# One fused attention and expert kernel: a new hand-written order of the work of eight images

## The reference

```python
x = x + conv(ln_c(x))            # attention block on the normed input
t = tokens(x)
t = t + ffn(ln_t(t))             # experts on the normed tokens

def conv(x):
    qkv = conv1x1(x)                         # 768 channels
    agg = grouped_1x1(depthwise_5x5(qkv))    # 25 taps per channel
    # 64 heads of 8 channels: 32 from qkv, 32 from agg
    q, k = relu(q), relu(k); v = [v, 1]
    kv = k^T v;  out = q kv;  out = out[:-1] / out[-1]
    return batchnorm(conv1x1(out))

def ffn(x):                                  # per image
    probs = softmax(mean_tokens(x) @ router)
    weights of 6 experts from the best 2 of 11 partitions
    return sum_e w_e * (gelu(x W1_e + b1_e) W2_e + b2_e)
```

## Time and profile before

| | us |
|---|---|
| median of 3 runs | 1727.04 |
| lowest and highest | 1724.31 and 1729.64 |
| the profiled execution | 1725.51 |
| its span, first to last instruction | 1723.6 |

### The profile page before, as it was taken

One profiled execution on the slowest core, in us unless ns is written; L12 is line 12 of the kernel. 1 busy time (PEld: TensorE's weight loads), 2 busy tenths in 40 slices (PEclk: granted clock), 3 DMA queues, 4 the chain that ended last, 5 costly groups with the idle time before them and its releaser, 6 DMA issues.

```text
span 1723.6 us, 18116 instructions
## 1 busy us (share of the span) xinstructions
PE 1403.7 (81%) x6652; PEld 771.5 (45%) x6652; DVE 1303.4 (76%) x1305; ACT 915.0 (53%) x1606; POOL 1187.4 (69%) x1017
## 2 busy tenths in 40 slices
PE   4344865988889878988889878988889879768998
PEld 2133534544545435544545435544445435534443
DVE  4999999889589895889589895889589895920000
ACT  3452642565557644665557645565557645433554
POOL 3673554877697758876697758876697757535776
PEclk7666986999999989999999989999999989988999
DMA  5100000000010000100010000100010000100000
GB/s 173 74 0 25 1 0 0 25 1 13 1 62 1 13 1 0 62 1 13 1 60 3 13 1 1 61 1 13 1 37 1 13 0 1 37 0 13 1 13 25
DMA packets 14247, 32.70 MB, mean 19 GB/s; under 512 B 2384, under 2 KB 5328, under 8 KB 13904
## 3 DMA queue, kind: packets, MB, share of 16 engines
q1 hardware_dynamic: 14160, 31.56, 5.2%
HBM read 23.17 MB, written 8.39 MB: 18 GB/s over the span
## 4 chain that ended last, share of the span: by engine, by line
PE 44%; DVE 23%; POOL 16%; ACT 10%; issue 6%; DMA 1%; POOLq 0%; SPq 0%; DVEq 0%
DVE dacc L1067 19%; PE wbk L487 16%; PE acc L500 12%; PE wbk L580 6%; POOL dwo L881 4%; POOL gl L915 3%; POOL hb L912 3%; ACT tapb L655 2%; POOL yr L905 2%; PE wbk L589 2%; PE wbk L534 2%; POOL nrm L838 1%; PE wbk L539 1%; PE wbk L554 1%; PE wbk L566 1%
## 5 line engine op out<-in xcount | busy, mean ns | idle before, releaser
L1067 DVE SCALAR_TENSOR_TENSOR dacc<-qkvs,dww,dacc 128x930 f32<-128x930 f32 (+4 forms) x954 | 1052.3, 1185 | 0.0
L912 POOL TENSOR_SCALAR hb<-hb,ewg 128x512 f32<-128x512 f32 x256 | 189.8, 742 | 252.2 <-ACT gh L677 252.1
L915 POOL TENSOR_TENSOR gl<-hb,gh 128x512 f16<-128x512 f32 x256 | 306.3, 1196 | 21.4
L770 ACT ACTIVATE hb<-wbk,b1s 128x512 f32<-128x512 f32 x256 | 175.4, 686 | 244.4 <-PE wbk L487 243.8
L881 POOL TENSOR_TENSOR dwo<-dwo,tapb 128x992 f32<-128x992 f32 (+1 forms) x104 | 237.4, 2283 | 46.7 <-ACT tapb L655 39.5
L487 PE MATMUL wbk<-th,w1h 128*128 128x512 f16 x512 | 163.8, 403 | 69.7 <-ACT vt L743 36.7
L500 PE MATMUL acc<-gh,w2h 128*128 128x512 f16 x512 | 200.6, 392 | 19.4 <-POOL gl L915 19.3
L677 ACT ACTIVATE gh<-hb,ewg 128x512 f16<-128x512 f32 x256 | 182.3, 712 | 40.7 <-DVE ewg L1020 40.7
L500 PE MATMUL acc<-gl,w2h 128*128 128x512 f16 x512 | 200.0, 391 | 0.0
L500 PE MATMUL acc<-gh,w2l 128*128 128x512 f16 x512 | 199.8, 390 | 0.0
L487 PE MATMUL wbk<-tl,w1h 128*128 128x512 f16 x512 | 162.3, 400 | 0.0
(11 more groups left out here) (147 smaller groups left out, 2388.7 us busy)
## 6 DMA issues: line engine op xcount, KB each, us to landing
xa<-x SPq DMA_DIRECT2D x8, 1024.0 KB, 5.0
yr<-x SPq DMA_DIRECT2D x8, 1024.0 KB, 5.0
out<-yr SPq DMA_DIRECT2D x16, 512.0 KB, 2.8
dwo<-w SPq DMA_DIRECT2D x1, 2048.0 KB, 10.9
yr<-w SPq DMA_DIRECT2D x2, 1024.0 KB, 16.0
dwo<-w_qkv SPq DMA_DIRECT2D x1, 768.0 KB, 4.7
wp<-w_proj SPq DMA_DIRECT2D x1, 512.0 KB, 12.1
pw<-w_pw SPq DMA_DIRECT2D x16, 24.0 KB
```

Of the source, the lines that this page charges most:

```text
L770: last = nc.scalar.activation(hb[:, f % GB, :], b[:], ACT.Gelu, bias=b1s[:, f % FT:f % FT + 1], scale=1.0 / (X_SCALE * W_SCALE))
L912: nc.gpsimd.tensor_scalar(hb[:, f % GB, :], hb[:, f % GB, :], ewg[s % 2][:, f % FT:f % FT + 1], 0.0, ALU.mult, ALU.add).then_inc(g_scaled, 1)
L915: nc.gpsimd.tensor_tensor(gl[:, f % GB, :], hb[:, f % GB, :], gh[:, f % GB, :], ALU.subtract).then_inc(g_low, 1)
L1067: ins = nc.vector.scalar_tensor_tensor(out=dst[:, oy, ox], in0=i3[:, jy, jx], scalar=dww[:, m, tap:tap + 1], in1=a3[:, oy, ox], op0=ALU.mu ...
```

## The change

Only the list, the items' grain and the places of the small tasks change; every instruction of the computation stays. `high`, `squares`, `relu_q`, `apply`, `low` and `scale` are split into one item for each block or half. `base` items are given one for each `fill` step (three after each banked item in j = 0). `gsplit` is given only once the image's `exp` is given, and so the first two steps of an image may come before its `exp`. The core of the new list:

```diff
+            if todo and ("low", todo[0][0], 1, CT - 1) in given and (("exp", todo[0][0]) in given or todo[0][1] < 2):
+                i = len(stream) - len(todo)
+                give(("ffn",) + todo.pop(0))
+                while unsplit and ("exp", unsplit[0][0]) in given:
+                    give(("gsplit",) + unsplit.pop(0))
+                unsplit.append(stream[i])
+                if i >= LAG:
+                    second(i - LAG)
+            base(1)
...
+    def norm_in(s):
+        return [[("squares", s, 0, 0)], [("squares", s, 0, 1), ("sums", s, 0)],
+                [("stats", s, 0, 0)], [("stats", s, 0, 1), ("rnorm", s, 0)],
+                [("rbc", s, 0, 0), ("rbc", s, 0, 1)], [("apply", s, 0, 0)], [("apply", s, 0, 1)]]
+    def norm_out(s):
+        return [[("high", s, 0, 0)], [("low", s, 0, 0), ("high", s, 0, 1)], [("low", s, 0, 1)]]
...
+    for j in range(B + 1):
+        d, c, a, f = j < B, j >= 1, j + 1 < B, j + 2 < B
+        new, nxt = j - 1, j + 1
         n = 3 if j == 0 else 1
         if c:
+            give(*agg(new, 0), *agg(new, 1))
+            fill(1)
             for t in range(TT):
+                give(("att", new, 1, t))
+                if t == 3:
+                    fill(1)
+                    give(("scale", new, 1, 0))
+            give(("scale", new, 1, 1))
+        if j == 0:
+            for group in norm_in(1)[:2]:
+                give(*group)
         if d:
+            give(*qkv(j, 0), *qkv(j, 1), n=n)
+            add_base(j, 0)
+            if j == 0:
+                for group in norm_in(1)[2:]:
+                    give(*group, n=n)
+        out = norm_out(nxt) if a else [[], [], []]
         if c:
+            fill(2)
+            give(*[("back", new, 1, ch, g) for ch in range(NCH) for g in range(2)])
+            fill(1)
+            give(("proj", new, 0, 0), *out[0])
+            give(("proj", new, 0, 1))
+            give(("proj", new, 1, 0), *out[1])
+            give(("proj", new, 1, 1))
+        else:
+            give(*out[0], *out[1])
+        toks = [("tok", j, t) for t in range(TT)] if d else []
+        give(*toks[:2], n=n)
+        if c:
+            if not d:
+                fill(2)
+            give(*out[2], ("squares", new, 1, 0))
+            give(*toks[2:4])
+            give(("squares", new, 1, 1), ("sums", new, 1))
+            give(*toks[4:])
+        else:
+            give(*out[2], *toks[2:], n=n)
         if d:
+            give(("relu_q", j, 0))
+            give(("kv", j, 0, 0), ("kv", j, 0, 1), n=n)
+            give(("mask", j, 0), ("relu_q", j, 1))
         if c:
+            fill(1)
+            give(("stats", new, 1, 0), ("rnorm", new, 1))
+            fill(1)
         if d:
+            give(*[("att", j, 0, t) for t in range(4)], n=n)
         if c:
+            fill(1 if d else 2)
+            give(("rbc", new, 1, 0), ("rbc", new, 1, 1), ("apply", new, 1, 0), ("apply", new, 1, 1))
+        if d:
+            give(("scale", j, 0, 0))
+            give(*[("att", j, 0, t) for t in range(4, TT)], n=n)
         if c:
+            give(("high", new, 1, 0))
+            fill(1 if d else 2)
+            give(("high", new, 1, 1))
+        if d:
+            give(("scale", j, 0, 1))
+        if c:
+            give(("low", new, 1, 0), ("low", new, 1, 1))
+            if a:
+                give(*qkv(nxt, 2))
+            give(("logits", new))
+        if d:
+            give(*[("back", j, 0, ch, g) for ch in range(NCH) for g in range(2)], n=n)
+        if c:
+            if a:
+                give(*qkv(nxt, 3))
+            else:
+                fill(1)
+            fill(left(new - 1) + 2)
             give(("exp", new))
...
+            give(*agg(j, 2), *agg(j, 3))
...
+            for group in norm_in(j + 2) if f else [[]] * 4:
+                give(*group)
+                fill(1)
+            fill(1)
+            give(*agg(j, 4))
+            fill(1)
+            give(*agg(j, 5))
+            fill(1)
+            if a:
+                for m in (4, 5):
+                    for it in qkv(nxt, m):
+                        give(it)
+                        fill(1)
+                add_base(nxt, 4)
+            else:
+                fill(4)
+            give(("kv", j, 1, 0))
+            fill(2)
+            give(("kv", j, 1, 1))
+            fill(1)
             give(("mask", j, 1))
+            while left(new) > KEEP and new >= 0:
+                fill(1)
...
+KEEP = 9
...
-            OF_LAST = {14: ("rden", 1, 0), 20: ("rden", 1, 1), 74: ("max",), 84: ("route",)}
-            OF_THIS = {94: ("rden", 0, 0), 100: ("rden", 0, 1)}
+            OF_LAST = {10: ("rden", 1, 0), 14: ("rden", 1, 1), 72: ("max",), 80: ("route",)}
+            OF_THIS = {58: ("rden", 0, 0), 64: ("rden", 0, 1)}
```

More of the change, by code:

```diff
@@ L82, in schedule @@
     o = []
+    given = set()
     waiting = []
@@ L85, in schedule, with give, base, rest @@
     todo = list(stream)
[L86 to L90, removed]
+    unsplit = []
+    def give(*items, n=1):
+        for it in items:
+            o.append(it)
+            given.add(it)
+            if it[0] in BANKED and n > 1:
+                base(n)
+    def base(n):
+        o.extend(waiting[:n])
+        del waiting[:n]
+    def rest():
+        base(len(waiting))
+    def add_base(s, a):
+        waiting.extend(("base", s, m, i) for m in (a, a + 1) for i in range(base_taps(s, m)))
     def second(k):
@@ L96, in second, with fill @@
             give(("final", s, n // FT))
-    def fill(k, s):
+    def fill(k):
         for _ in range(k):
[L100 to L130, removed]
@@ new lines, in norm_out @@
+    def norm_out(s):
+        return [[("high", s, 0, 0)], [("low", s, 0, 0), ("high", s, 0, 1)], [("low", s, 0, 1)]]
+    give(("squares", 0, 0, 0), ("squares", 0, 0, 1), ("sums", 0, 0), ("weights", 0), ("stats", 0, 0, 0),
+         ("stats", 0, 0, 1), ("rnorm", 0, 0), ("rbc", 0, 0, 0), ("rbc", 0, 0, 1), ("apply", 0, 0, 0),
+         ("apply", 0, 0, 1), ("weights", 1), ("high", 0, 0, 0), ("low", 0, 0, 0), ("high", 0, 0, 1), ("low", 0, 0, 1))
+    give(*[it for m in range(2, QT) for it in qkv(0, m)])
@@ L135, in schedule @@
+    add_base(0, 2)
+    add_base(0, 4)
+    for j in range(B + 1):
+        d, c, a, f = j < B, j >= 1, j + 1 < B, j + 2 < B
+        new, nxt = j - 1, j + 1
         n = 3 if j == 0 else 1
         if c:
-            agg(new, 0)
-            fill(1, old)
+            give(*agg(new, 0), *agg(new, 1))
+            fill(1)
             for t in range(TT):
[L140 to L143, removed]
@@ L179, in schedule @@
-        if c:
-            give(("exp", new))
-        fill(2, new)
-        if a:
-            based([("stats", j + 1, 0, i) for i in range(2)])
-            give(("rnorm", j + 1, 0))
-            fill(2, new)
-            based([("rbc", j + 1, 0, ch) for ch in range(NCH)])
-            give(("apply", j + 1, 0))
-        if j == -1:
-            give(("weights", 1))
-        if d:
[L191 to L194, removed]
-            give(("scale", j, 0))
@@ new lines, in schedule @@
+        if d:
[6 more added lines that the diff above has]
+            fill(left(new - 1) + 2)
+            give(("exp", new))
+        rest() if j == 0 else None
+        if d:
+            give(*agg(j, 2), *agg(j, 3))
+            if a and c:
+                add_base(nxt, 2)
+        if j == 0:
+            give(*qkv(1, 2), *qkv(1, 3))
+            add_base(1, 2)
@@ L223, in schedule @@
     return o
+KEEP = 9
+BANKED = ("qkv", "agg", "kv", "stats", "rbc", "att", "back", "proj", "tok", "logits", "ffn")
 ORDER = schedule()
-BANKED = ("qkv", "agg", "kv", "stats", "rbc", "att", "back", "proj", "tok", "logits", "ffn")
 FILL = {it: n for n, it in enumerate([it for it in ORDER if it[0] in BANKED])}
@@ L243, in norm_before @@
 def norm_before():
-    runs = [(it[1], it[2]) for it in ORDER if it[0] == "squares"]
+    runs = [(it[1], it[2]) for it in ORDER if it[0] == "squares" and it[3] == 0]
     return dict(zip(runs[1:], runs))
```

141 lines of the change are left out of this document (47 added, 94 removed).

## The result

The new list takes 1774.07 us (1770.77 to 1776.88, four runs), the old one 1727.11 beside it: ratio 1.0272, 95% interval 1.0248 to 1.0296. It is 2.7% slower. The forecast was 1708, and the range ended at 1742.

The account below looks back on a forecast made before the run. Bound: a PE-ACT-POOL loop of fixed-order queues, with VectorE hung on it at the logits. 228 + 187 + 4 x 195 + 175 + 165 + 170 = 1705 us of span, plus 1.9 and 1.5: 1708; range 1640 to 1742.

Parts of the forecast that it names:

- Stage A: From agg of q to the logits: 83 us, against 105.7 before; the wait before `max` goes.
- Stage B: From the logits to the routed weights: 22.5 us, ending at 105.5 in the period; 20.3 before.
- head: Start to the end of the first image's taps: 228 us, against 201.8, as VectorE stands 26 us at `rden`.
- light period: First period after the head, without old steps: 187 us, VectorE's taps setting the route at 100.7.
- j = 7: Last tap period, without qkv or norm: 165 us, against 183.7 before.
- tail: Behind the last tap period, with 9 steps of image 6 left instead of 22: 170 us, against 204.7.
- stage C: From routed weights to the input norm's rbc: 26.5 us, POOL's serial queue making PE stand at three places.
- Rival 2: The slower rival: the stretch behind the route costs more, through half clock, 6 us a period; 1738 us; chance 0.26.
- The third rival: Logits come no earlier; Stage A costs 4 us more in each of four periods; 1724, no change; chance 0.10.
- Stage D: From rbc to the next agg of q: 58.7 us, plus 2.5 for half clock and 1.8 for taps; period 195.
- The period of j = 6: The period without an input norm: 20 us shorter for the norm's missing work, 175 us.
- the rival of the experiments that named PE's clock: Set up for the experiments: PE's own number of items and clock set the period; no size or chance given.

Follow-up runs that it names:

- run 3: Kernel after, with no base items at the steps between the input norm's groups (j of 1 and more): 1729.01 us.
- run 5: Kernel after with the edits of run 1 and run 3, and no base item at the three steps around the last kv items: 1700.59 us.
- run 6: Kernel of run 5, with the input norm's squares and sums moved ahead of the last old steps and exp: 1671.43 us.
- Run 9: Kernel before, with the next image's squares and sums moved behind exp and the new image's first two steps, from j = 1: 1758.74 us.
- run 10: Kernel after, with only the input norm's squares and sums moved ahead of the last old steps and exp; base items stay: 1751.99 us.
- run 2: Kernel after, with the input norm's squares and sums given right behind exp, ahead of the two early gsplits: 1755.42 us median.
- run 1: Kernel after, with image 0's two reciprocal tasks back before taps 94 and 100: 1759.93 us.

## Why the prediction was wrong

**What was right.** Stage A: 86.5 us from agg of q to the logits, forecast 83. Stages A and B together 105.5, as forecast to the tenth, if by errors that cancel (below). `max` waits no more, VectorE stands 29.9 us in the first image (26) and about 34 in each steady period (some 20), three waits for POOL of 2.5, 4.1 and 5.1 us lie behind exp (5, 5 and 6). The head came at 232.2 (228), the light period at 190.5 (187), j = 7 at 165.6 (165), the tail at 173.2 (170). The rival that named the right sign and one of the two places, stage C, was the second one, and its threshold was passed: the period is above 200. But it priced the head and the periods at 30 us in all, for the clock alone, and the runs are 66 above the forecast. The third rival's size came true too, stage A cost 3.5 us more than I said (it had put 4); no run divides that.

**What failed: the size of stages C and D.** The mechanism held; what was mis-sized is the time in which POOL's queue holds PE behind the route. The forecast put a period at 195, the runs at 204.8. Over the four periods (the first was 207.6) that is 42 us of the 70 by which the span is above the forecast's 1705; j = 6 is 16, the rest 12. By terms:

- Stage C, 33 and not 26.5. (a) I let the first gsplit follow the weights by 0.7 us, as in the earlier trace rows; here it comes 3.5 behind (940.76 to 944.29), as ScalarE has agg's copies, a square, a table load and a gelu in front. That is 2.8. No run tested it by itself. (b) One square's sum took 3.33 and a gsplit 1.66 beside a pair of VectorE taps, 1.9 together. I had put that 1.8 in the period's sum, not in this stage. (c) rbc itself ran at half clock, 3.52 us instead of 1.9.
- Stage D, 66.4 and not 58.7 with 4.3 for clock and taps. I allowed 2 us of POOL waits and there are 7.9: 2.25, 1.95 and 3.74. The list puts a base with each step, so that a step with an `apply` costs POOL 0.69 + 1.16 + 2.31 + 2.37 = 6.5 us, against 2.59 of PE's pace, and near the end final, base and mask, 6.2 us, stand ahead of one gsplit. I had summed POOL up to rbc item by item, and stopped there. Runs 3 and 5 put a price on the base items: about 7 us a period for those among the norm's steps (of stages C and D together), 3.6 for those near the end.
- Stage B in turn was 3.5 shorter than I said (19.0 instead of 22.5), mainly because the route took VectorE 3.4 us, not 8.4: the 8.4 had been measured beside a busy POOL, and my own text had POOL idle there.

Together, with stage A, +3.5 - 3.5 + 6.5 + 3.4 = 9.9, the miss of a period.

**The period of j = 6.** I took 20 us off for the missing norm and got 175; it measured 191.2. About 10 of the 16 are the period's own miss; the rest is the 20, for the period is only 13.7 shorter than its neighbours (204.9). I subtracted the norm's work from a period in which PE had been waiting for it. With the norm gone PE waits for `gl` instead, seven times, 13.3 us in all, because that period keeps its base items and finals. Run 3 brings it to 182.5.

**The reasoning on the old list.** I took 5.1 and 1.9 us for the base backlog at agg of q as a gain that the new list would keep. The wait at agg of q is gone from PE's list, but the new list paid more for the same items elsewhere. What I did not ask was where the moved items go on POOL, step by step, through the whole period. That the order ahead of the route matters, and that POOL stands there idle, was in my own text ("The list of before put squares and sums ahead of the first gsplit"); the slower rival got 0.26. Runs 6 and 9 move the same items in opposite directions, in two lists, and give 29 us less and 33 us more.

**The clock.** 4.4 of the 10.3 us a period are PE busy for longer with the same matmuls. I had 2.5. Rival 2 gave 6 for it. Waits and slow clock come together, but in no fixed measure: from after to run 6 the standing falls by 11.0 us a period and the busy time by 6.1; of this run 3 alone has 6.6 and only 0.5, the step from run 5 to 6 has 3.2 and 4.2. So the rival of the experiments that named PE's clock is right in part: an edit that moves POOL's work changes the period by standing and by clock, and no run parts the two.

## What to carry to other kernels

Where several engines follow one list, sum the slowest helper's queue over every step of a period, not only over the stretch that looks critical; an item that is moved is paid where it lands. Work that does not depend on a late result (here the norm's sums) belongs ahead of the wait for it, where the helper stands anyway, and deferrable work (base taps) belongs neither behind that wait nor past its own due time. And to subtract an operation that the bound engine was waiting for, redo the sum without it; what stood beside it is what remains. A duration taken beside a busy neighbour is no price for a place where that neighbour stands.

## What the runs showed of the hardware

**One list, two speeds.** In run 10 one period follows another with the same waits of PE, and they differ by 5.0 us. All of it is PE's busy time and clock:

```profile
618.20:817.10 198.90, 172.12 (x829) 95.47 (x828) 159.41 (x161) 112.55 (x200) 141.79 (x122) 0.93 0.05 16
817.10:1021.00 203.90, 177.31 (x830) 98.45 (x829) 159.40 (x161) 112.67 (x200) 146.64 (x128) 0.90 0.05 16
```

Run 9 does the like, 201.4 and 198.0, and run 2 has executions 11 us apart. What makes the granted clock (1.00 is 2.4 GHz) come back sooner in one period than in the other was not tested. An effect of 2 or 3 us a period can't be read from a single period.

**VectorE's small operations.** The route took 8.4 us between 1066.6 and 1075.0 in the kernel before and 3.4 in the kernel after (937.34 to 940.76), with the same instructions. In the first POOL works through most of it; in the second it stands idle from 935.6 to 944.3. VectorE and POOL in the kernel before:

```profile
1067.34 2.03 DVE L995 TENSOR_SCALAR rt<-rt 128x2 f32<-128x2 f32 x1
1069.40 2.94 DVE L998 TENSOR_SCALAR wsel<-iota,rt 128x11 f32<-128x11 f32 x2
```

```profile
1067.00 2.34 POOL L810 TENSOR_TENSOR rb<-xa 128x1024 f32<-128x1024 f32 x1
1069.31 2.34 POOL L812 TENSOR_TENSOR nrm<-nrm 128x1024 f32<-128x1024 f32 x1
1071.63 0.68 POOL L912 TENSOR_SCALAR hb<-hb,ewg 128x512 f32<-128x512 f32 x1
```

In the kernel after the same ones took 0.23 us (L1039) and 0.49 for the two (L1042). In the kernel before L995 ends at 1069.37, just as POOL's L810 does (1069.34), and L998 at 1072.34, just as L912 does (1072.31). So these rows fit small VectorE operations that wait until POOL's running instruction is done, and they hold 4.3 of the 5.0 us of difference. No run changed only this.

**Taps and POOL.** Beside the pair of first taps at 951.98, which took 5.37 us for two, the sum took 3.33 and the gsplit 1.66, together 1.9 over their usual time. The second row is a first tap of run 1 with POOL idle:

```profile
951.98 5.37 DVE L1103 SCALAR_TENSOR_TENSOR dacc<-qkvs,dww,dwo 128x1024 f32<-128x1024 f32 x2
```

```profile
199.52 1.29 DVE L1104 SCALAR_TENSOR_TENSOR dacc<-qkvs,dww,dwo 128x1024 f32<-128x1024 f32 x1
```

Both sides lose. The ends fit instructions that take turns: POOL's L857 ends at 952.98, then the first tap can run and the sum behind it is 1.0 late; the sum ends at 956.26, the second tap 1.1 behind it at 957.35, and the gsplit is 1.0 late. The Trainium skill ("SBUF — State Buffer", Who interferes with whom) has the VectorE instruction with two SBUF inputs contend with a POOL one that reads SBUF, through a port pair that works as an exclusive lock; by this trace that holds. The 3.6 us that I had weighed against my 1.8 came from two taps of 1.8 each, and those 1.8 already held the taps' own waits for POOL: alone they are 2 x 1.29, and they held POOL for 1.9.
